# A routed expert stage with 16 pairs of tiles and 7 single tiles in place of 12 and 15

## The reference, cut to what matters

```python
xf = x.reshape(-1, D)                                   # 2048 x 256, after a layer norm
sh = gelu(einsum('nd,sdh->snh', xf, sw1) + sb1)         # S = 2 shared experts, hidden 512
shared_out = (einsum('snh,shd->nd', sh, sw2) + sb2.sum(0)) / S
topv, topi = top_k(xf @ router_w + router_b, 2)         # E = 8 routed experts, 2 per token
probs = softmax(topv)
y = einsum('enh,ehd->end', gelu(einsum('nd,edh->enh', xf, w1) + b1), w2) + b2
x = x + tanh(g_ffn) * (shared_out + sum over the two chosen experts of probs * y)
```

## Time and profile before

| what | us |
| --- | --- |
| median of three runs | 381.22 |
| lowest and highest run | 380.16, 381.27 |
| span of the profiled execution | 378.1 |
| TensorE busy in it | 370.8 |
| VectorE, ScalarE, GpSimd busy in it | 282.0, 241.7, 221.4 |

### The profile page before, as it was taken

One profiled execution on the slowest core, in us unless ns is written; L12 is line 12 of the kernel. 1 busy time (PEld: TensorE's weight loads), 2 busy tenths in 40 slices (PEclk: granted clock), 3 DMA queues, 4 the chain that ended last, 5 costly groups with the idle time before them and its releaser, 6 DMA issues.

```text
span 378.1 us, 8799 instructions
## 1 busy us (share of the span) xinstructions
PE 370.8 (98%) x2773; PEld 352.3 (93%) x2774; DVE 282.0 (75%) x612; ACT 241.7 (64%) x540; POOL 221.4 (59%) x262
## 2 busy tenths in 40 slices
PE   8999999999999999999999999999999999999996
PEld 7898989999999989999999999999999997999995
DVE  5798799978988988799898897555556555554486
ACT  3666545665665545787878757766666665777850
POOL 8367657688878764377885226546565655653200
PEclk9999999999999999999999999999999999999999
DMA  7990000001000048511940022222223233650397
GB/s 219 313 340 6 2 14 29 16 21 35 14 14 14 29 142 333 222 32 14 300 138 2 14 46 84 80 63 85 83 79 89 85 84 111 210 144 30 110 350 251
DMA packets 33839, 40.15 MB, mean 106 GB/s; under 512 B 9674, under 2 KB 26508, under 8 KB 33676
## 3 DMA queue, kind: packets, MB, share of 16 engines
q1 hardware_dynamic: 28960, 29.40, 25.0%
q0 software_dynamic: 4768, 10.28, 8.9%
q10 hardware_dynamic: 76, 0.02, 0.0%
HBM read 27.88 MB, written 11.68 MB: 105 GB/s over the span
## 4 chain that ended last, share of the span: by engine, by line
PE 91%; DVE 2%; POOL 2%; issue 2%; DMA 1%; ACT 1%; DVEq 0%; POOLq 0%
PE psum L1336 12%; PE psum L1359 12%; PE psum L1296 10%; PE psum L1252 10%; PE psum L1504 8%; PE psum L1598 8%; PE psum L1478 6%; PE psum L1559 6%; PE psum L1219 3%; PE psum L1138 2%; PE psum L1176 2%; PE psum L1200 2%; PE psum L1583 2%; PE psum L1284 1%; PE psum L1491 1%
## 5 line engine op out<-in xcount | busy, mean ns | idle before, releaser
L743 POOL DMA_INDIRECT y_tok<-ysl,table x39 | 38.9, 996 | 41.7 <-ACT ysl L1029 36.5
L736 POOL DMA_INDIRECT xsl<-y_rows,table x39 | 38.7, 991 | 30.0 <-PE psum L1359 9.6
L709 POOL DMA_INDIRECT names<-named,pos x32 | 37.5, 1170 | 12.8 <-issue 7.9
L662 POOL TENSOR_TENSOR Eb<-Eb,rinv 128x512 f32<-128x512 f32 x32 | 33.5, 1065 | 13.1 <-DVE rinv L1810 13.1
L1073 ACT ACTIVATE hr<-psum,b_cur 128x256 f32<-128x256 f32 x48 | 20.1, 470 | 22.1 <-DVE b_cur L2103 12.3
L905 ACT ACTIVATE yTb<-psum 128x256 f32<-128x256 f32 x16 | 6.2, 385 | 42.7 <-PE psum L1316 42.7
L1598 PE MATMUL psum<-xsT_hi,w_cur 128*128 128x256 f32 x192 | 31.0, 284 | 0.0
L645 POOL TENSOR_TENSOR half_sum<-Eb 128x512 f32<-128x512 f32 x16 | 20.6, 1287 | 12.0 <-ACT Eb L860 11.8
L1598 PEld LDWEIGHTS psum<-xsT_hi,w_cur 128*128 128x128 f32 x192 | 26.5, 192 | 0.0
L2152 DVE TENSOR_TENSOR hr_lo<-hr,hr_hi 128x512 fp32r<-128x512 f32 x24 | 16.6, 692 | 13.2 <-ACT hr_hi L1086 13.0
L940 ACT ACTIVATE early_stage<-psum,vec_col 128x256 f32<-128x256 f32 x48 | 20.0, 467 | 8.8 <-PE psum L1336 8.0
(11 more groups left out here) (276 smaller groups left out, 1255.9 us busy)
## 6 DMA issues: line engine op xcount, KB each, us to landing
w_raw<-in_L_ffn_w SPq DMA_DIRECT2D x2, 4096.0 KB, 15.6
y_got<-y_tok SPq DMA_DIRECT2D x8, 512.0 KB, 8.3
xs_all<-in_x SPq DMA_DIRECT2D x4, 512.0 KB, 12.3
sw_raw<-in_L_ffn_sw SPq DMA_DIRECT2D x2, 1024.0 KB, 13.8
y_rows<-ybuf SPq DMA_DIRECT2D x16, 128.0 KB, 1.7
sw_lo_kept<-sw_lo SPq DMA_DIRECT2D x1, 2048.0 KB, 6.6
sw_lo<-sw_lo_kept SPq DMA_DIRECT2D x8, 256.0 KB, 3.1
out<-xs_all SPq DMA_DIRECT2D x3, 512.0 KB, 3.1
```

Source lines behind the costliest of these rows:

```text
L662: nc.gpsimd.tensor_tensor(Eb[q][:, heads, :], Eb[q][:, heads, :], rinv[:, q, heads].unsqueeze(2).broadcast_to([P, H // 2, CTX]), ALU.mult) ...
L709: nc.gpsimd.indirect_dma_start(names, bass.IndirectOffsetOnAxis(ap=pos[:, k, t:t + 1], axis=0), named[:, k, t, :], None).then_inc(scattere ...
L736: nc.gpsimd.indirect_dma_start(into[:, s % 2, :], None, y_rows, bass.IndirectOffsetOnAxis(ap=table[:, s, 0:1].bitcast(I32), axis=0)).then_ ...
L743: nc.gpsimd.indirect_dma_start(y_tok, bass.IndirectOffsetOnAxis(ap=table[:, s, 1:2].bitcast(I32), axis=0), ysl[:, s % 2, :], None).then_in ...
```

## The change

`DOUBLES` becomes 16 and `DOUBLE0` 4, so `SINGLES` is 7: four singles, 16 pairs (places 4 to 35), three singles (36 to 38). Places of pairs that no pair needs take an odd last tile, at most one per expert, which takes seven more small instructions in the routing chain. The two copies for the first pair move from single 3 to single 1, those for the second to singles 2 and 3. The rests come back under waits of their own: four pieces of the first weights from the last pair but one on, four of the second during the last three singles; TensorE waits for the first four before the shared first layer and for the others only before its second.

```diff
-DOUBLES = (TOK * TOPK // P - E) // 2
+DOUBLES = TOK * TOPK // P // 2
 SINGLES = SLOT_TILES - 2 * DOUBLES
-DOUBLE0 = 6
+DOUBLE0 = 4
 SINGLE1 = DOUBLE0 + 2 * DOUBLES
...
-                n = s - (SLOT_TILES - BACK)
-                if n >= 0:
-                    for i in range(2):
-                        if i == 0:
-                            sp.wait_ge(h_psum, SINGLE1 + n)
-                        else:
-                            sp.wait_ge(ht_psum, SINGLE1 + n + 1 - 2 * DOUBLES)
-                        piece = slice((2 * n + i) * SW_WORDS // BACK, (2 * n + i + 1) * SW_WORDS // BACK)
-                        sp.dma_start(sw_s[1][:, piece].bitcast(F32), sw_lo_kept[:, piece]).then_inc(sw_moved, 16)
...
+            for n in range(2):
+                sp.wait_ge(h_psum, SINGLE1 - 2 + n)
+                bring_back(n, sw1_back)
+            sp.wait_ge(h_psum, SINGLE1)
+            bring_back(2, sw1_back)
+            bring_back(3, sw1_back)
+            for n in range(2):
+                sp.wait_ge(ht_psum, DOUBLE0 + 1 + n)
+                bring_back(4 + 2 * n, sw2_back)
+                sp.wait_ge(h_psum, SINGLE1 + 2 + n)
+                bring_back(5 + 2 * n, sw2_back)
...
+            for s in range(tile_of(2)):
+                gather(s)
+            scatter(0)
+            scatter(1)
+            for d in range(2, 4):
+                for n in range(2):
+                    gather(tile_of(d) + n)
+                scatter(d)
             for d in range(1, DOUBLES):
...
-            pe.wait_ge(sw_moved, 16 + 32 * BACK)
+            pe.wait_ge(sw1_back, 16 * BACK)
             hidden(EARLY, late, range(0, 1))
...
             pe.wait_ge(ye_ready, SLOT_TILES)
+            pe.wait_ge(sw2_back, 16 * BACK)
             project(EARLY, late)
...
-            in_pairs = run_e[1 - f][:, 1, :]
-            link(nc.vector.tensor_scalar(in_pairs[:, PADE:], pairs, float(DOUBLES), 2.0, ALU.min, ALU.mult))
-            link(nc.vector.tensor_tensor(ends_s[:, :], ends, in_pairs[:, PADE:], ALU.subtract))
+            held, in_pairs = (run_e[1 - f][:, i, :] for i in range(2))
+            link(nc.vector.scalar_tensor_tensor(odd[:, :], pairs, -2.0, ends, ALU.mult, ALU.add))
+            link(nc.vector.tensor_scalar(pairs, pairs, float(DOUBLES), None, ALU.min))
+            link(nc.vector.tensor_scalar(spare[:, :], pairs[:, E - 1:E], -1.0, float(DOUBLES), ALU.mult, ALU.add))
+            link(nc.vector.tensor_scalar(odd[:, :], odd[:, :], spare[:, 0:1], None, ALU.min))
+            link(nc.vector.tensor_tensor(in_pairs[:, PADE:], pairs, odd[:, :], ALU.add))
+            link(nc.vector.tensor_scalar(in_pairs[:, PADE:], in_pairs[:, PADE:], 2.0, None, ALU.mult))
+            link(nc.vector.tensor_tensor(held[:, PADE:], ends, odd[:, :], ALU.add))
+            link(nc.vector.tensor_tensor(ends_s[:, :], held[:, PADE:], in_pairs[:, PADE:], ALU.subtract))
             link(nc.vector.tensor_tensor(two_u[:, :], in_pairs[:, PADE:], in_pairs[:, PADE - 1:PADE + E - 1], ALU.subtract))
             link(nc.vector.tensor_scalar(unused[:, 1, :], two_u[:, :], -1.0, float(NT), ALU.mult, ALU.add))
-            link(nc.vector.tensor_scalar(unused[:, 0, :], tiles_e[:, :], -1.0, float(NT), ALU.mult, ALU.add))
+            link(nc.vector.tensor_tensor(unused[:, 0, :], held[:, PADE - 1:PADE + E - 1], held[:, PADE:], ALU.subtract))
+            link(nc.vector.tensor_scalar(unused[:, 0, :], unused[:, 0, :], float(NT), None, ALU.add))
             link(nc.vector.tensor_tensor(unused[:, 0, 0:E - 1], unused[:, 0, 0:E - 1], two_u[:, 1:E], ALU.add))
```

More of the change, by code:

```diff
@@ L169, in build @@
          iota_e, iota_tile, iota_slot, oh, chosen, run_a0, run_a1, run_b0, run_b1, run_e0, run_e1, full_tile, tiles_e,  tot, place, picked, pos_f, passed,
-         emap_f, first_row, unused, two_u, ends_s, moved, moved_f, val, idx, prob, dif, ex, den, mv1, ve1, ra, rq, rb, r1, mx, sm, rinv, lg, v8, i8), end = row_of(scratch, [
+         emap_f, first_row, unused, two_u, ends_s, odd, spare, moved, moved_f, val, idx, prob, dif, ex, den, mv1, ve1, ra, rq, rb, r1, mx, sm, rinv, lg, v8, i8), end = row_of(scratch, [
              ("vec_rows", [NVEC, P], F32), ("cvec_rows", [NCVEC, CK], F32),
@@ L308, in build @@
         xsl2_loaded = [sem(f"xsl2_loaded{i}") for i in range(2)]
-        half_used, sw_moved = (sem(n) for n in ("half_used", "sw_moved"))
+        half_used, sw_moved, sw1_back, sw2_back = (sem(n) for n in ("half_used", "sw_moved", "sw1_back", "sw2_back"))
         w1_moved = sem("w1_moved")
@@ L409, in experts, with of, fetch_pair @@
             regs = [eng.alloc_register(f"expert{n}") for n in range(IN_FLIGHT)]
+            pair_regs = [eng.alloc_register(f"pair_expert{n}") for n in range(2)]
+            def of(reg):
+                return eng.snap(reg, min_val=0, max_val=E - 1)
             def fetch(n, q):
                 eng.load(regs[n % IN_FLIGHT], emap[0:1, at(q)])
-            return (lambda n: eng.snap(regs[n % IN_FLIGHT], min_val=0, max_val=E - 1)), fetch
+            def fetch_pair(par, q):
+                eng.load(pair_regs[par], emap[0:1, at(q)])
+            return (lambda n: of(regs[n % IN_FLIGHT])), fetch, (lambda par: of(pair_regs[par])), fetch_pair
         def routed(eng, step, double, before={}):
@@ L747, in _ @@
                 pool.wait_ge(kept, 16 * NT // 2)
-            gather(0)
-            gather(1)
-            for s in range(DOUBLE0):
-                if s + 2 < DOUBLE0:
-                    gather(s + 2)
-                if s >= DOUBLE0 - 2:
-                    gather(s + 4)
-                if s >= 3:
-                    scatter(s - 3)
-                if s in (2, 3):
-                    gather(s + 4)
-            scatter(DOUBLE0 - 3)
-            for n in range(2):
-                gather(tile_of(2) + n)
-            scatter(DOUBLE0 - 2)
-            for n in range(2):
-                gather(tile_of(3) + n)
-            scatter(DOUBLE0 - 1)
+            for s in range(tile_of(2)):
[6 more added lines that the diff above has]
+                scatter(d)
             for d in range(1, DOUBLES):
@@ L1468, in turn, with give @@
                 last.then_inc(xt_psum, 1)
-            def give(s, par, u):
+            def give(s, par):
                 pe.wait_ge(ht_lo, s + 1)
@@ L1495, in give_wide @@
             def give_wide(s, n):
-                e = expert(n)
+                e = pair_expert(n)
                 pe.wait_ge(ye_ready, s)
@@ L1575, in step @@
                         pe.wait_ge(acc_free, EARLY * TPS + 2)
-                    give(s - 2, par, s - 2)
+                    give(s - 2, par)
                 if s < 2:
@@ L1605, in double @@
                     turn_wide(xsl, xsl_loaded, 16 * (DOUBLE0 // 2 + 1), s + 2, 1)
-                    give(DOUBLE0 - 2, 0, DOUBLE0 - 2)
-                    fetch(0, entry(tile_of(0)))
-                    give(DOUBLE0 - 1, 1, DOUBLE0 - 1)
+                    give(DOUBLE0 - 2, 0)
+                    fetch_pair(0, entry(tile_of(0)))
+                    give(DOUBLE0 - 1, 1)
                 elif d == DOUBLES - 1:
                     fetch(SINGLE1, entry(SINGLE1))
-                    fetch(1, entry(s))
+                    fetch_pair(1, entry(s))
                     turn(SINGLE1, 0)
@@ L1620, in double @@
                     give_wide(s - 2, 1 - par)
-            expert, fetch = experts(pe)
+            expert, fetch, pair_expert, fetch_pair = experts(pe)
             fetch(0, 0)
@@ L2181, in late_start @@
                 add_step(EARLY - 1)
-            expert, fetch = experts(dve)
+            expert, fetch, pair_expert, fetch_pair = experts(dve)
             fetch(0, 0)
```

29 lines of the change are left out of this document (16 added, 13 removed).

## The result

The changed kernel takes 382.61 us (median of six runs, 381.94 to 385.23), the kernel before 381.17 us on the same device (379.56 to 381.51). The ratio is 1.0057, with a 95% interval from 1.003 to 1.0084: it is slower by 1.1 to 3.2 us. The forecast was 380.2 us, faster by 1.0, with a range to 381.4; it was wrong in sign, and the time lies outside the range.

What follows compares the result with a forecast made beforehand. TensorE, busy 370.8 of 378.1 us, was taken to bound the kernel. Terms -3.1 + 0.9 + 0.8 + 0.4 = -1.0 us took 381.2 to 380.2 us, with an 8-in-10 range of 378.5 to 381.4.

Steps and rivals of the forecast that it cites:

- the loss among the first pairs: Wide phase: four pairs took 25.56 us where 4 x 6.19 is 24.76; this 0.8 us stays, nothing new.
- wide phase's feed: Rival: the 0.8 us among the first pairs vanishes or comes twice, giving 379.4 or 381.0 us; chance 0.14.
- The saving: Routed stage on TensorE: eight singles become four pairs, fewer transposes of hidden rows, 3.1 us less.
- The routing: Thirteen links for six delay VectorE 1.5 us; TensorE starts block 3's late columns 0.9 us late.
- The copies: Single 1: two weight copies ahead of `late_start` make TensorE 0.8 us late at single 2's second layer.
- Place 36's gather: First single after the pairs: gather beside one returning piece lands after 4.5 us against 4.1 of cover, costing 0.4 us.
- the gap that I had named as a sign: Expected TensorE gap before the transposes of place 36, ending with its gather.
- The two VectorE terms: TensorE delays from VectorE's late work: 0.9 us at the routing and 0.8 us at single 1's copies.

Runs made afterwards that it cites:

- e1: Changed kernel with GpSimd's two gathers issued ahead of the two scatters in the wide phase: 380.84 us, ratio 1.0011.
- e13: Changed kernel with gathers before scatters, late_start before the copies, block 3's columns first after routing, rests together after place 36's transposes: 378.58 us, ratio 0.9949.
- e18: Kernel of e13 with the rests brought back as in the changed kernel: 379.97 us, ratio 0.9965.
- e4: Kernel before, still 12 pairs, with the change's thirteen small routing instructions in place of six: 381.4 us, ratio 1.0024.
- e17: Kernel before with two small GpSimd memsets between the two gathers of a pair: 380.85 us, ratio 0.9994.
- e3: Changed kernel with late_start ahead of the first pair's two weight copies in single 1: 381.21 us, ratio 1.0027.
- e15: Changed kernel with all eight pieces of the rests issued together after place 36's rows are transposed: 382.26 us, ratio 1.0041.
- e16: Changed kernel with a small VectorE memset ahead of the copy of the high weights in pairs: 382.26 us, ratio 1.0061.
- e14: Kernel before with one small GpSimd memset between the two gathers of a pair: 380.81 us, ratio 0.9999.

## Why the prediction was wrong

**The step that failed.** It is this one: "The order of GpSimd's queue from there on is the old one two places earlier, so I also keep the loss among the first pairs: [...] 0.8 us, which stays and costs nothing new." The order is the same, yet the loss became 2.85 us. In place of a fixed price there is a feedback: the second gather is issued behind two scatters and a first gather, its rows arrive only 0.4 us before TensorE wants them (in the kernel before, issued at 272.00, landing after 2.8 us, wanted at about 275.2), and 0.5 us of extra time on GpSimd passes this cover. Before, the pairs settled where the gather starts as `hr_lo` ends and the copy begins, and lost nothing more; after, they went back and forth between 0.07 us into the copy and 0.10 us into `hr_lo`, both of which make the gather long. That the loss hangs on the gathers' place behind the scatters is shown by e1, e13 and e18, in all of which the pairs take 6.21 us; that the longer gather sets it off is read from the rows, not tested. A single long gather isn't enough: behind the first stall, the next second gather took 1.37 and 1.45 us in e4 and e17, and two pairs later both were at 0.96, while e3, e15 and e16 had 0.96 there and 1.45 to 1.47 two pairs later. All four undisturbed profiles with 16 pairs and the old order of gathers and scatters (after, e3, e15, e16) fall into the losing pattern, and none of the four with 12 pairs (before, e4, e14, e17) does. Whether the number of leading singles, the number of pairs or something else decides it stays open. The rival "wide phase's feed" named the right place, but priced it at one more stall of 0.8 us, because I had the row of a gather's landing and not its distance from the need in every pair.

**The saving**, 3.1 us: right. A pair with nothing to wait for takes 6.19 us in the changed kernel too (242.32 to 248.51), the narrow products are no dearer than before (2.88 us for 24), and e13's stage comes out with this 3.1 in it, as accounted above.

**The routing**, 0.9 us: right in mechanism, a little large. Thirteen links took 176.66 - 173.98 = 2.68 us, 0.21 each. They run from the first row here, on VectorE's timeline, to the second:

```profile
173.98 0.17 DVE L2022 SCALAR_TENSOR_TENSOR odd<-run_e 128x8 f32<-128x8 f32 x1
...
176.66 0.23 DVE L2038 TENSOR_TENSOR passed<-iota_slot,ends_s 128x49 f32<-128x49 f32 x1
...
184.69 0.68 DVE L1861 TENSOR_TENSOR early_cols_lo<-yT,early_cols_hi 128x512 fp32r<-128x512 f32 x1
```

The same rest of block 3's columns came 2.2 us later, 0.95 of it with everything, and TensorE's first product at 185.43 in place of 183.87, 1.56 later: 0.6 net there, with about 0.1 more in products that ran long around it. It came in two gaps, one where TensorE waits for the adding of block 1 as well, which I had folded into one.

**The copies**, 0.8 us: right in place, 1.05 in size. `late_start` now stands behind both copies, on VectorE's timeline:

```profile
227.94 0.69 DVE L2123 CAST w_cur<-w_hi 128x1024 fp32r x1
228.55 0.68 DVE L2123 CAST w_cur<-w_lo 128x1024 fp32r x1
229.15 0.87 DVE L1972 SCALAR_TENSOR_TENSOR xs_all<-psum,half_tg,xs_all 128x256 f32<-128x256 f32 x2
```

It starts 1.21 us later against the single than before, just as worked out. TensorE's gap is 0.72 us; the other 0.3 are in its 12 products behind it, 1.75 us in place of 1.44. I had no term for that.

**Place 36's gather**, 0.4 us: the sum was right by accident. It was issued at 330.27, and TensorE turned its rows at 334.54 without waiting, so it landed within 4.3 us and cost nothing; the gap that I had named as a sign isn't there. GpSimd's timeline and TensorE's:

```profile
330.27 0.98 POOL L752 DMA_INDIRECT xsl<-y_rows,table  x1 [0.30 <-issue]
```

```profile
334.54 0.38 PE L1473 MATMUL psum<-ident,xsl 128*128 128x128 f32 x2
```

What cost 0.4 us was the scatter of place 34 beside the returning rests, in the chain of waits: ScalarE may not write the next result until it has landed.

```profile
346.14 3.46 DMA y_tok<-ysl,table
...
352.73 1.73 PE psum L1484 x12
```

The two VectorE terms missed by 0.2 us one way and by 0.25 the other, and the third 0.4 us came from another cause than the one named; that the three still add up to what was forecast for them is luck. The sum with the measured terms and the failed one is -3.1 + 0.7 + 1.05 + 0.4 + 2.05 = +1.1 us, and the timed medians differ by 1.44. Without the failed term it would have been -0.95, the forecast. The range was too narrow because it let the wide phase vary by 0.8 us either way, when every second pair could lose 0.44.

## What to carry to other kernels

In a loop, price not only what an edit adds but how close the loop's slowest feed comes to its need: a distance of 0.4 us in a pair of 6.19 is a loss waiting for a change of phase, and it is multiplied by the trips. Put loads that someone waits for ahead of stores in a shared queue, but look where the stores go then: here, with the gathers first and nothing else altered, 2.6 us were gained among the pairs, and new waits of 0.70 and 1.18 us for a gather and a store came up behind them. An instruction added to shift a phase has to be seen to shift it before its time says anything.

## What the runs showed of the hardware

A GpSimd gather that took 0.96 us took up to 1.47 when it started just after a VectorE instruction of 0.69 us that reads no PSUM. It grew by the rest of that instruction less 0.13 us, within 0.04 us in 166 cases; beside instructions that read PSUM it did not grow (0.94 to 0.99). Between two gathers GpSimd has 0.30 us in which one or two small instructions (0.12 us each) cost nothing. A VectorE memset of 0.06 us, which the profile has 0.03 us behind the copy's start, did not delay the copy (0.61 us behind `hr_lo` with and without it). Beside eight pieces of 256 KB issued together a gather landed after 6.9 us (6.2 in e13) in place of 2.8, later than the 5.0 beside two pieces.
